# Routing the last attention batch in two halves, and ending three stages without a semaphore clear and a GpSimd drain

## The chip, the cores and the metric

The kernel is one program on one core of one Trainium2 chip. The core has TensorE (PE, with its weight loads as PEld), VectorE (DVE), ScalarE (ACT), GpSimd (POOL) and SyncE (SP), which run their own instruction streams and meet only at semaphores, and 16 DMA engines. The metric is the device time of one execution in microseconds (us), as the median of several executions; lower is better.

## The reference

Four batches (B = 4) of 1024 tokens with 256 features go through two layers. In each layer a mixer and a mixture of experts are added to the residual stream, with adaptive layer norms before them. The stages that matter here are the attention of the second layer and the routing of its experts:

```python
h = _layernorm(x) * (1 + ca) + sa
x = x + ga * _L1_attn_ref(h, Wqkv, Wo)          # 8 heads of 128, causal
h = _layernorm(x) * (1 + cb) + sb
x = x + gb * _L1_ffn_ref(h, gate_w, w1, w2)     # 16 experts, top 2, capacity 640 rows

# _L1_ffn_ref, in flat token order over all batches:
probs = jax.nn.sigmoid(xf @ gate_w.T)
top_vals, sel = jax.lax.top_k(probs, 2)
weights = top_vals / (top_vals.sum(-1, keepdims=True) + 1e-06)
ranks = (running count of each expert's tokens, in token order) - 1
valid = ranks < capacity                         # later ones are dropped
slot = jnp.where(valid, sel * capacity + ranks, sentinel)
padded = zeros.at[slot].set(x_rep)               # a row of x for each of its 2 experts
out = (gathered expert outputs * weights).sum(axis=1)
```

A token's slot depends on how many earlier tokens chose the same expert, so the tiles of 128 tokens are ranked in order.

## The kernel before

The program is five stages, each a block of its own in which every engine has its stream: the first layer's mixer (`phase_mamba`), its routing (`phase_route`), its experts (`phase_experts0`), the second layer's attention (`phase_attention`) and its experts (`phase_experts1`). A block ends with a barrier of all engines. In the built program each engine drains before the barrier, POOL among them. The semaphores of a stage are taken through the class `Semaphores`, whose exit (lines 75 and 76) has POOL drain and clear their range, and then has all engines meet at another barrier. Four single semaphores that outlive a stage (`xo_`, `rm_`, `aw_`, `ew_`) have such an object each. At the end of `phase_experts0` two ranges are cleared one after the other, at the end of `phase_attention` one, and at the program's end four.

Attention takes the batches one by one. Tokens lie in tiles of 128 on the partitions, so a batch has TPB = 8 tiles, and CT = 4 of them are half a batch. A batch's 8 heads of 8 tiles are 64 steps, in whose loop the other work has fixed places: the next batch's norms, and the routing of the previous batch (constants `R_NORM`, `R_PAIR`, `PICK`, `RANK`, `SLOTS`). After the steps come the eight output tiles (`output(t)` on PE, line 1879), which DVE scales, adds to x and takes statistics of (lines 2232 to 2236).

The last batch has no successor to hide its routing under. What follows its output tiles is, in this order:

- DVE: `variance` over 8 tiles (lines 2039 to 2045), ACT's square root (1945), `invert`, and two instructions for each of 8 rows tiles (`route_row`, lines 2059 and 2062).
- PE and ACT in turn, for each of four pairs of tiles: `turn_pair` (1797) transposes into the one bank `qk_ps`, ACT copies (1949), `logits` (1805) go into the same bank, ACT takes exp (1954). The next pair waits for that.
- DVE: `pick` twice (2082 to 2093), which gives two experts a token; PE: `count_before` (1812, 1813); DVE: `weights`, `take_ranks`, `slots` (2102 to 2121).
- POOL: 16 indirect DMAs, two for each tile, which scatter the rows into `slots1` (1757), then a wait until they have landed.

Only then does the block end and `phase_experts1` begin: SP loads the gates and the rows of expert 0 (1461, 1467), PE transposes them (1506) and works through 16 experts (1517, 1528), and POOL adds each tile of results to `out` by an indirect DMA (1494).

## Time and profile before

| | us |
|---|---|
| median of 3 timed runs | 2989.36 (2987.97 to 2989.59) |
| the profiled execution's own time | 2964.37 |
| span of its trace, first to last instruction | 2962.6 |
| last batch's output tiles end on PE | 2573.2 |
| first scatter issue of the last batch | 2607.16 |
| first instruction of the last stage | 2635.17 |
| mean granted TensorE clock over the span | 0.922 |

All rows in this text are from the one profiled execution, in us from the start of its span. The names before an instruction's operands are tiles (`at_` is attention's, `e_` the experts'), `<-` stands between what is written and what is read, and a bracket at a row's end is the time that the engine sat idle before it and what ended that. The letter q behind an engine's name stands for its instruction queue: a `DRAIN` there waits for what its engine has under way, a `COMPARE_BRANCH` or `UNCONDITIONAL_BRANCH` is the way out of a block, and it starts when the wait before it is met. The clock column PEclk gives 1.00 for 2.4 GHz and 0.50 for 1.2 GHz.

### The profile page before, as it was taken

The page shows a single profiled execution, that of the slowest core. Times are in us where ns is not written, and L with a number is a line of the kernel's source. Part 1 is how long each engine was busy: PE and PEld are TensorE (multiplying, and loading weights), DVE is VectorE, ACT ScalarE, POOL GpSimd, SP SyncE. Part 2 cuts the span into 40 slices and gives each one's busy share as a digit, 9 for nine tenths or more (in the row PEclk, how much of TensorE's full clock was granted, in tenths as well). Part 3 has the DMA queues.
Part 4 walks back from the last instruction along what each step waited for, and adds up shares of the span by engine and source line. Part 5 has one row for each costly group of instructions (what it writes and reads, how often), then busy time and mean ns, then how long its engine had stood idle before and what let it go on. Part 6 is the DMA issues. An engine that isn't in the chain of part 4 may idle for free. (4 is left out here: it accounts for less than half of the span.)

```text
span 2962.6 us, 39492 instructions
## 1 busy us (share of the span) xinstructions
PE 2504.5 (85%) x12433; PEld 1817.4 (61%) x12434; DVE 2100.9 (71%) x4243; ACT 1286.0 (43%) x2525; POOL 1241.6 (42%) x531
## 2 busy tenths in 40 slices
PE   6677877877856859998799999999999999839998
PEld 4355555555545859997466665666566666627776
DVE  4999999999998456665666567757675677435554
ACT  4667777777754215554243323323332343201111
POOL 2799999999997036665000000020002001123434
PEclk8889989988977579999799999999999999869999
DMA  4645654654654434343300010001001000035554
GB/s 145 203 152 173 198 169 168 192 175 161 200 179 149 139 112 63 63 63 53 118 1 1 1 47 1 1 30 33 1 1 47 1 1 13 32 95 127 126 128 73
DMA packets 151034, 269.21 MB, mean 91 GB/s; under 512 B 18348, under 2 KB 107484, under 8 KB 150364
## 3 DMA queue, kind: packets, MB, share of 16 engines
q1 hardware_dynamic: 121916, 227.12, 24.1%
q0 software_dynamic: 28416, 38.05, 7.8%
q10 hardware_dynamic: 544, 2.10, 0.2%
q8 instruction: 80, 1.31, 0.2%
q14 instruction: 78, 0.64, 0.1%
HBM read 209.65 MB, written 57.56 MB: 90 GB/s over the span
## 5 line engine op out<-in xcount | busy, mean ns | idle before, releaser
L765 POOL TENSOR_TENSOR dbx<-u,b_all 128x2048 f32<-128x2048 f32 x128 | 578.4, 4532 | 71.2 <-DVE u L844 34.2
L1757 POOL DMA_INDIRECT slots<-at_r_rows,slot_of x64 | 63.6, 994 | 1154.5 <-DVE slot_of L2121 1136.2
L649 ACT ACTIVATE da_ps<-delta,a_neg 128x512 f32<-128x512 f32 x512 | 347.9, 689 | 134.8 <-DVE hc L917 126.7
L1986 ACT COPY at_pt<-at_pt_ps 128x512 f32<-128x512 f32 (+3 forms) x384 | 171.8, 484 | 498.3 <-PE at_pt_ps L1858 498.1
L469 PE MATMUL y_ps<-ident,hc 128*128 128x128 f32 x1536 | 241.7, 301 | 90.8 <-DVE hc L917 90.3
L1847 PE MATMUL at_s_ps<-at_qk 128*128 128x512 f32 (+3 forms) x768 | 291.3, 489 | 3.1 <-DVE at_v L2170 3.1
L1871 PE MATMUL at_o_ps<-at_pt,at_v 128*128 128x512 f32 (+3 forms) x768 | 288.4, 487 | 0.0
L469 PEld LDWEIGHTS y_ps<-ident,hc 128*128 128x128 f32 x1536 | 196.0, 155 | 145.0 <-DVE hc L917 117.6
L1975 ACT ACTIVATE at_probs<-at_s_ps,at_small 128x128 f32<-128x128 f32 (+7 forms) x256 | 192.3, 751 | 206.2 <-DVE at_small L2181 205.8
L917 DVE TENSOR_TENSOR hc<-da_ps,c_all 128x512 f32<-128x512 f32 x384 | 257.5, 672 | 0.0
L907 DVE TENSOR_TENSOR_SCAN da_ps<-da_ps,state,dbx 128x512 f32<-128x512 f32 x192 | 243.1, 1276 | 6.1 <-ACT da_ps L649 4.3
L907 DVE TENSOR_TENSOR_SCAN da_ps<-da_ps,dbx 128x512 f32<-128x512 f32 x192 | 232.0, 1218 | 11.4 <-ACT da_ps L649 7.8
L1847 PEld LDWEIGHTS at_s_ps<-at_qk 128*128 128x128 f32 x768 | 136.9, 190 | 126.9 <-issue 94.9
L1831 PE MATMUL at_qk_ps<-at_h_b,w_qkv 128*128 128x512 f32 x448 | 211.9, 595 | 1.5 <-DVE at_rank L2107 0.9
L2177 DVE TENSOR_TENSOR at_s_ps<-at_s_ps,at_later 128x128 f32<-128x128 f32 x256 | 75.9, 296 | 186.5 <-PE at_s_ps L1847 185.5
L1494 POOL DMA_INDIRECT out<-e_ys,e_row_i x80 | 125.3, 1566 | 193.4 <-DVE e_ys L1603 164.5
L2179 DVE TENSOR_REDUCE at_small<-at_s_ps 128x1 f32<-128x128 f32 (+7 forms) x256 | 194.0, 758 | 8.8
L1858 PEld LDWEIGHTS at_pt_ps<-ident,at_probs 128*128 128x128 f32 x1152 | 136.2, 141 | 74.5 <-issue 49.6
L1858 PE MATMUL at_pt_ps<-ident,at_probs 128*128 128x128 f32 x1152 | 168.7, 273 | 11.4 <-DVE at_probs L2189 11.1
L1551 ACT ACTIVATE e_hid<-e_h_ps 128x320 f32<-128x320 f32 x128 | 56.0, 437 | 249.2 <-PE e_h_ps L1517 249.2
L1871 PEld LDWEIGHTS at_o_ps<-at_pt,at_v 128*128 128x128 f32 x768 | 127.2, 191 | 60.1 <-issue 56.6
L1528 PE MATMUL e_y_ps<-e_w,e_hid 128*128 128x256 f32 x640 | 152.3, 382 | 5.6 <-ACT e_hid L1551 5.6
(325 smaller groups left out, 5064.7 us busy)
## 6 DMA issues: line engine op xcount, KB each, us to landing
b_all<-bc_rows SPq DMA_DIRECT2D x128, 512.0 KB, 4.6
c_all<-bc_rows SPq DMA_DIRECT2D x128, 512.0 KB, 5.1
e_w<-L_ffn_w SPq DMA_DIRECT2D x32, 512.0 KB, 5.4
slots<-zeros SPq DMA_DIRECT2D x40, 260.0 KB, 6.3
e_xs<-slots SPq DMA_DIRECT2D x16, 650.0 KB, 7.1
w<-L_ffn_W SPq DMA_DIRECT2D x24, 384.0 KB, 8.6
more<-zeros SPq DMA_DIRECT2D x16, 256.0 KB, 5.2
sums<-x SPq DMA_DIRECT2D x8, 512.0 KB, 7.1
```

What stands on the lines that cost most here:

```text
L469: mm = nc.tensor.matmul(y_ps[par][:, at], source[:, at], sh.ident[:], start=False, stop=(last and j == CT - 1), is_transpose=True)
L649: nc.scalar.activation(da_ps[s % RING_DA][:], delta[:, c % 2, m, :], ACT.Exp, scale=sh.a_neg[:, m, n:n + 1]).then_inc(S["da_ready"], 1)
L765: nc.gpsimd.tensor_tensor(dbx[:, at % RING_DBX], pair, rows, ALU.mult).then_inc(S["dbx_ready"], 1)
L907: nc.vector.tensor_tensor_scan(out, h, dbx[:, at % RING_DBX, i // 2, par, :], 0.0 if c % CPB == 0 else state[:, s:s + 1], ALU.mult, ALU.ad ...
L917: nc.vector.tensor_tensor(hc[:, v % RING_H, :], da_ps[s % RING_DA][:], c_all[:, at % RING_C, s % GS // 2, :], ALU.mult).then_inc(S["hc_rea ...
L1831: last = nc.tensor.matmul(out, w_qkv[:, k, h, i // 2, :], h_b[:, i % 2, k, :], start=(k == 0), stop=(k == KE - 1))
L1847: last = nc.tensor.matmul(s_ps[n % 2][:, part * CH:end], qk[:, h % 2, 0, i * P:(i + 1) * P], qk[:, h % 2, 1, part * CH:end], start=True, s ...
L1858: last = nc.tensor.transpose(pt_ps[half][:, j % CT, :], probs[:, n % 3, j * P:(j + 1) * P], sh.ident[:])
L1871: last = nc.tensor.matmul(o_ps[:, first:], v[:, h % 2, j, :], pt[half][:, j, first:], start=(j == 0), stop=(j == (half + 1) * CT - 1))
L1975: nc.scalar.activation(probs[:, n % 3, 0:(i + 1) * P], s_ps[n % 2][:, 0:(i + 1) * P], ACT.Exp, bias=small[:, n % 4, 1:2], scale=SCALE, acc ...
L1986: nc.scalar.copy(pt[i // CT][:, half * CT:half * CT + m, at], pt_ps[half][:, 0:m, :]).then_inc(S[f"copied{half}"], 1)
L2179: nc.vector.reduce_max(small[:, n % 4, 0:1], s_ps[n % 2][:, 0:(i + 1) * P], AX_X).then_inc(S["max_taken"], 1)
```

## The change

It has two parts. The first is in `phase_attention`: `variance`, `invert`, `route_row`, `pick`, `weights`, `take_ranks` and `slots` of the last batch are replaced by functions that handle half a batch (four tiles), called `tail_*`. The first half's normalised rows, transposes and logits stand between the last output tiles; the second half follows them. Transposes go into the two banks `pt_ps`, in turn, the copies into `rows`, the logits of two pairs side by side into `qk_ps`, and the counts into `o_ps`. POOL's scatter waits for each half by itself. Three small POOL instructions prepare a constant `run_on4`. The first three batches are handled as before.

The second part: the semaphores of the last three stages and the four single ones are all taken from one object made in `program`, which clears them at the end of the program, and the blocks of these three stages are made with `no_gpsimd_drain=True`.

```diff
 program():
+        kept = ctx.enter_context(Semaphores(nc, ""))
+        sh.kept = lambda prefix: lambda name: kept(prefix + name)
-            sh.x_stored = ctx.enter_context(Semaphores(nc, "xo_"))("stored")
+            sh.x_stored = sh.kept("xo_")("stored")
...
-            sh.e0_w_in = second_block.enter_context(Semaphores(nc, "ew_"))("loaded")
+            sh.e0_w_in = sh.kept("ew_")("loaded")
 phase_experts0(), phase_experts1(), phase_attention():
-        sem = ctx.enter_context(Semaphores(nc, "at_"))
+        sem = sh.kept("at_")
-        block = ctx.enter_context(nc.Block())
+        block = ctx.enter_context(nc.Block(no_gpsimd_drain=True))
 phase_attention(), gpsimd:
-            def scatter(rb):
-                pool.wait_ge(S["slots_ready"], rb + 1)
-                for j in range(TPB):
+            def scatter(rb, tiles=range(TPB), count=None):
+                pool.wait_ge(S["slots_ready"], count or rb + 1)
+                for j in tiles:
...
-            scatter(B - 1)
+            for half in range(2):
+                scatter(B - 1, range(half * CT, (half + 1) * CT), B + half)
 tensor:
+            def tail_turn(pair):
+                pe.wait_ge(S["tail_row"], 4 * pair + 4)
+                if pair >= 2:
+                    pe.wait_ge(S["tail_copied"], pair - 1)
+                for j in range(2):
+                    for k in range(KE):
+                        last = nc.tensor.transpose(pt_ps[pair % 2][:, j * KE + k, :], r_rows[:, 2 * pair + j, k * P:(k + 1) * P], sh.ident[:])
+                last.then_inc(S["tail_turned"], 1)
+
+            def tail_logits(half):
+                if half:
+                    pe.wait_ge(S["tail_chance"], 1)
+                for pair in (2 * half, 2 * half + 1):
+                    pe.wait_ge(S["tail_copied"], pair + 1)
...
+            def tail_count(half):
+                pe.wait_ge(S["tail_masks"], half + 1)
+                if half:
+                    pe.wait_ge(S["tail_ranks"], 1)
+                pairs = both[:, half * CT:(half + 1) * CT, :]
+                nc.tensor.matmul(o_ps[:, 0:CT * NE], tri[:], pairs, start=True, stop=True)
+                nc.tensor.matmul(o_ps[:, CT * NE:2 * CT * NE], ones[:], pairs, start=True, stop=True).then_inc(S["tail_ranked"], 1)
...
                     output(t)
+                    if last_batch and t == TPB - 3:
+                        tail_turn(0)
+                    if last_batch and t == TPB - 2:
+                        tail_turn(1)
+                        tail_logits(0)
+                if last_batch:
+                    tail_count(0)
+                    tail_turn(2)
+                    tail_turn(3)
+                    tail_logits(1)
+                    tail_count(1)
 scalar:
+            for half in range(2):
+                nc.scalar.preload_act_table_set("sqrt_and_others")
+                tail_root(half)
+                nc.scalar.preload_act_table_set("exp_and_others")
+                for pair in (2 * half, 2 * half + 1):
+                    tail_copy(pair)
+                tail_chance(half)
 vector:
+                def tail_slots(half):
...
+                    tail_link(v.tensor_tensor(c, r, offs[:].rearrange("p (o e) -> p o e", o=1).broadcast_to([P, CT, NE]), ALU.add))
+                    tail_link(v.tensor_scalar(valid4, r, float(CAP1), None, ALU.is_lt))
+                    tail_link(v.scalar_tensor_tensor(out=c, in0=c, scalar=spare[:, 0:1], in1=valid4, op0=ALU.subtract, op1=ALU.mult))
+                    for k in range(2):
+                        tail_link(v.tensor_tensor(scores[:, at], mask[:, k, at], c, ALU.mult))
+                        tail_link(v.tensor_reduce(slot[:, k, at], scores[:, at], AX_X, ALU.add))
+                    tail_link(v.tensor_scalar(slot[:, :, at], slot[:, :, at], spare[:, 0:1], None, ALU.add))
+                    v.tensor_copy(sh.slot_of[:, :, b * TPB + half * CT:b * TPB + (half + 1) * CT], slot[:, :, at]).then_inc(S["slots_ready"], 1)
...
                     nc.vector.bn_stats(sh.stats[:, tile, :], sh.x[:, tile, :]).then_inc(S["stats2_in"], 1)
+                    if last_batch:
+                        if t == CT - 1:
+                            tail_variance(0)
+                        if t in (CT, CT + 1):
+                            tail_row(2 * (t - CT))
+                            tail_row(2 * (t - CT) + 1)
+                        if t == TPB - 2:
+                            tail_pick(0)
+                if last_batch:
+                    tail_variance(1)
+                    for j in range(CT, TPB):
+                        tail_row(j)
+                    tail_weights(0)
+                    tail_slots(0)
+                    tail_pick(1)
+                    tail_weights(1)
+                    tail_slots(1)
-            variance(B - 1, "2")
-            invert(B - 1, "2")
-            for j in range(TPB):
-                route_row(B - 1, j)
-            pick(B - 1, 0)
-            pick(B - 1, 1)
-            weights(B - 1)
-            take_ranks(B - 1)
-            slots(B - 1)
```

How the instructions stand now, first on TensorE from output tile 2 of the last batch to the end of the stage. `at_s_ps<-at_w_o,at_attn` is an output tile (8 matmuls), `at_r_rows` a transposed row tile, `at_gate_w` the logits, `at_tri` and `at_ones` the counts. Before:

```order
L1879 MATMUL at_s_ps<-at_w_o,at_attn 128x256 x48
L1797 MATMUL at_qk_ps<-ident,at_r_rows 128x128 x4
L1805 MATMUL at_qk_ps<-at_gate_w,at_gated 128x16 x4
L1797 MATMUL at_qk_ps<-ident,at_r_rows 128x128 x4
L1805 MATMUL at_qk_ps<-at_gate_w,at_gated 128x16 x4
L1797 MATMUL at_qk_ps<-ident,at_r_rows 128x128 x4
L1805 MATMUL at_qk_ps<-at_gate_w,at_gated 128x16 x4
L1797 MATMUL at_qk_ps<-ident,at_r_rows 128x128 x4
L1805 MATMUL at_qk_ps<-at_gate_w,at_gated 128x16 x4
L1812 MATMUL at_qk_ps<-at_both,at_tri 128x128
L1813 MATMUL at_qk_ps<-at_both,at_ones 128x128
L1632 UNCONDITIONAL_BRANCH
```

And now:

```order
L1914 MATMUL at_s_ps<-at_w_o,at_attn 128x256 x32
L1828 MATMUL at_pt_ps<-ident,at_r_rows 128x128 x4
L1914 MATMUL at_s_ps<-at_w_o,at_attn 128x256 x8
L1828 MATMUL at_pt_ps<-ident,at_r_rows 128x128 x4
L1839 MATMUL at_qk_ps<-at_gate_w,at_rows 128x16 x8
L1914 MATMUL at_s_ps<-at_w_o,at_attn 128x256 x8
L1847 MATMUL at_o_ps<-at_both,at_tri 128x64
L1848 MATMUL at_o_ps<-at_both,at_ones 128x64
L1828 MATMUL at_pt_ps<-ident,at_r_rows 128x128 x8
L1839 MATMUL at_qk_ps<-at_gate_w,at_rows 128x16 x8
L1847 MATMUL at_o_ps<-at_both,at_tri 128x64
L1848 MATMUL at_o_ps<-at_both,at_ones 128x64
```

The transposes of the first pair stand ahead of output tile 6, those of the second pair and the logits of both ahead of output tile 7, and each half has its counts.

Second, DVE around the last output tile (`at_gated<-at_s_ps,mods` takes it, `BN_STATS` ends it). Before:

```order
L2232 TENSOR_TENSOR at_gated<-at_s_ps,mods 128x256
L2234 TENSOR_TENSOR x<-x,at_gated 128x256
L2236 BN_STATS stats<-x 128x6
L2232 TENSOR_TENSOR at_gated<-at_s_ps,mods 128x256
L2234 TENSOR_TENSOR x<-x,at_gated 128x256
L2236 BN_STATS stats<-x 128x6
L2039 TENSOR_TENSOR mean<-stats 128x8
L2040 TENSOR_SCALAR mean<-mean 128x8
```

And now, from the fourth row before it:

```order
L2325 SCALAR_TENSOR_TENSOR at_cand<-at_cand,at_iota_e 128x64
L2326 TENSOR_REDUCE at_idx<-at_cand 128x4
L2327 TENSOR_TENSOR at_mask<-at_iota_e,at_idx 128x64
L2331 TENSOR_TENSOR at_both<-at_mask 128x64
L2376 TENSOR_TENSOR at_gated<-at_s_ps,mods 128x256
L2378 TENSOR_TENSOR x<-x,at_gated 128x256
L2380 BN_STATS stats<-x 128x6
L2293 TENSOR_TENSOR mean<-stats 128x4
L2294 TENSOR_SCALAR mean<-mean 128x4
```

The first half's 14 instructions of `pick` (the last four are shown) stand between output tiles 6 and 7, and the statistics are those of four tiles.

Third, POOL from the last batch's scatter to the end of the program's stages. `L75 ISA` is the clear of a range of semaphores, a branch the end or the start of a block. Before, from the end of attention:

```order
L1632 UNCONDITIONAL_BRANCH [waits ss_own_kept]
L75 ISA [waits barrier_Pool_Activation_PE_DVE_SP_gather]
L1482 UNCONDITIONAL_BRANCH [waits barrier_Pool_Activation_PE_DVE_SP_gather]
L1484 IOTA e_expert 128x16
L1486 IOTA e_spare 128x5
```

And now, from the first half's last seven scatters (the semaphore's number has another first owner, whose name is shown):

```order
L1763 DMA slots<-at_r_rows,slot_of 10368x260 x7
L1763 DMA slots<-at_r_rows,slot_of 10368x260 [waits ss_zeros_set]
L1763 DMA slots<-at_r_rows,slot_of 10368x260 x7
L1632 UNCONDITIONAL_BRANCH [waits ss_ident_set]
L1482 UNCONDITIONAL_BRANCH [waits barrier_Pool_Activation_PE_DVE_SP_gather]
L1484 IOTA e_expert 128x16
L1486 IOTA e_spare 128x5
```

The clear between the two branches has gone, as have the two at the end of `phase_experts0`; at the program's end one `L75 ISA` stands where there were four. That clear keeps the drain of POOL that comes with it (line 75).

## Rows read from the trace of the kernel before

**Rows 1.** Windows: us, busy time (instructions) by engine, clock, DMA share, GB/s.
```profile
2540.00:2573.00 33.00, 33.00 (x144) 26.82 (x142) 9.63 (x22) 0.60 (x1) 0.00 (x0) 1.00 0.00 0
...
2601.00:2642.00 41.00, 0.01 (x1) 0.01 (x1) 6.32 (x23) 1.28 (x1) 15.59 (x18) 0.50 0.27 94
2642.00:2657.00 15.00, 14.23 (x44) 9.31 (x44) 8.70 (x28) 3.12 (x8) 0.00 (x0) 0.72 0.59 196
```

**Rows 2.** Timeline, end of attention: start, us, engine, line, instruction, idle before it.
```profile
2573.22 0.42 DVE L2232 TENSOR_TENSOR at_gated<-at_s_ps,mods 128x256 f32<-128x256 f32 x1 [2.11 <-PE at_s_ps L1879]
...
2574.60 0.17 DVE L2039 TENSOR_TENSOR mean<-stats 128x8 f32<-128x8 f32 x1
...
2576.57 0.48 DVE L2059 SCALAR_TENSOR_TENSOR at_r_rows<-x,mean,mods 128x256 f32<-128x256 f32 x1
...
2583.51 0.48 DVE L2062 SCALAR_TENSOR_TENSOR at_r_rows<-at_r_rows,rstd,mods 128x256 f32<-128x256 f32 x1
...
2594.40 0.23 DVE L2082 TENSOR_SCALAR at_chances<-at_chances 128x128 f32<-128x128 f32 x1 [10.40 <-ACT at_chances L1954]
2594.66 0.95 DVE L2083 RECIPROCAL at_chances<-at_chances 128x128 f32<-128x128 f32 x1
...
2599.21 0.29 DVE L2093 TENSOR_TENSOR at_both<-at_mask 128x128 f32<-128x128 f32 x1
...
2601.10 0.29 DVE L2102 COPY at_plus<-at_qk_ps 128x128 f32<-128x128 f32 x1
...
2606.71 0.17 DVE L2121 CAST slot_of<-at_slot 128x16 uint32<-128x16 f32 x1
2607.16 0.96 POOL L1757 DMA_INDIRECT slots<-at_r_rows,slot_of  x1 [78.34 <-DVE slot_of L2121]
...
2626.12 0.96 POOL L1757 DMA_INDIRECT slots<-at_r_rows,slot_of  x1 [0.30 <-issue]
```

**Rows 3.** Line 1632, attention's block end: queue records, ns min/median/max, start.
```profile
L1632 POOLq COMPARE_BRANCH  x1: 43/43/43, 2628.7 to 2628.7; - x1
L1632 POOLq DRAIN  x1: 5279/5279/5279, 2628.8 to 2628.8; - x1
...
L1632 SPq EVENT_SEMAPHORE  x1: 17/17/17, 2634.3 to 2634.3; - x1
```

**Rows 4.** Line 1224, the block end of `phase_experts0`.
```profile
L1224 POOLq COMPARE_BRANCH  x1: 44/44/44, 1400.8 to 1400.8; - x1
L1224 POOLq DRAIN  x1: 4464/4464/4464, 1400.9 to 1400.9; - x1
```

**Rows 5.** Line 1421, the block end of `phase_experts1`.
```profile
L1421 POOLq COMPARE_BRANCH  x1: 41/41/41, 2956.3 to 2956.3; - x1
L1421 POOLq DRAIN  x1: 4137/4137/4137, 2956.5 to 2956.5; - x1
```

**Rows 6.** Timeline, starts of the last two stages.
```profile
1406.93 0.37 SPq L1697 DMA_DIRECT2D x<-sums  x1
...
2635.17 0.34 SPq L1461 DMA_DIRECT2D mods<-mod_rows  x1
...
2639.43 1.10 DVE L1610 TENSOR_TENSOR mods<-mods 128x256 f32<-128x256 f32 x3 [32.55 <-DMA mods<-mod_rows]
```

**Rows 7.** Line 75, the nine semaphore clears, each with its drain.
```profile
L75 POOLq DRAIN  x9: 41/89/174, 973.3 to 2962.2; - x9
L75 POOLq EVENT_SEMAPHORE_RANGE_CLEAR  x9: 44/131/461, 973.5 to 2962.2; - x9
```

**Rows 8.** Timeline, TensorE routing a pair inside the last batch, at clock 1.00.
```profile
2465.00 0.60 PE L1797 MATMUL at_qk_ps<-ident,at_r_rows 128*128 128x128 f32 x4
2466.94 0.96 PE L1805 MATMUL at_qk_ps<-at_gate_w,at_gated 128*128 128x16 f32 x8
```

**Rows 9.** Timeline, first and last of 16 scatter issues while DVE is busy.
```profile
2508.51 0.96 POOL L1757 DMA_INDIRECT slots<-at_r_rows,slot_of  x1 [266.28 <-DVE slot_of L2121]
...
2527.86 0.96 POOL L1757 DMA_INDIRECT slots<-at_r_rows,slot_of  x1 [0.30 <-issue]
```

More of the change, by code:

```diff
@@ L1651, in phase_attention @@
         r_turned = gated[:].rearrange("p j (k t) -> p j k t", k=KE)
+        tail_rows = rows[:].rearrange("p (h j) (k t) -> p h j k t", h=2, k=KE)
         s_ps = [ps(f"s_ps{i}", [P, T]) for i in range(2)]
@@ L1928, in batch @@
                     output(t)
-            batches(pe, batch)
-            for pair in range(PAIRS):
-                if pair:
-                    pe.wait_ge(S["chances_ready"], (B - 1) * PAIRS + pair)
-                turn_pair(B - 1, pair)
-                logits(B - 1, pair)
-            pe.wait_ge(S["chances_ready"], B * PAIRS)
-            count_before(B - 1)
+                    if last_batch and t == TPB - 3:
[9 more added lines that the diff above has]
+                    tail_count(1)
+            batches(pe, batch)
         @block.scalar
@@ L2005, in _, with tail_root, tail_copy, tail_chance @@
             batches(act, batch)
-            root(B - 1, "2")
-            for pair in range(PAIRS):
-                copy_pair(B - 1, pair)
-                chance(B - 1, pair)
+            def tail_root(half):
+                act.wait_ge(S["tail_var"], half + 1)
+                at = slice((B - 1) * TPB + half * CT, (B - 1) * TPB + (half + 1) * CT)
+                nc.scalar.activation(sh.var[:, at], sh.var[:, at], ACT.Sqrt).then_inc(S["tail_std"], 1)
+            def tail_copy(pair):
+                act.wait_ge(S["tail_turned"], pair + 1)
+                if pair >= 2:
+                    act.wait_ge(S["tail_logits"], 1)
+                nc.scalar.copy(tail_rows[:, pair % 2], pt_ps[pair % 2][:].rearrange("p (j k) t -> p j k t", j=2)).then_inc(S["tail_copied"], 1)
+            def tail_chance(half):
+                act.wait_ge(S["tail_logits"], half + 1)
+                at = slice(half * CT, (half + 1) * CT)
+                nc.scalar.activation(chances[:, at, :], qk_ps[:, 0:CT * NE].rearrange("p (j e) -> p j e", j=CT), ACT.Exp, scale=-1.0).then_inc(S["tail_chance"], 1)
+            for half in range(2):
[5 more added lines that the diff above has]
+                tail_chance(half)
         @block.vector
```

98 lines of the change are left out of this document (90 added, 8 removed).

## The prediction

> **What bounds the kernel now.** The span is a chain of five stages, so I read first, by windows, what each engine does around the last stage change. Up to 2573 TensorE is busy for all of 33.00 us at a granted clock of 1.00 (2.4 GHz). From 2601 to 2642 it does nothing for 41 us, while POOL is busy for 15.59 us [rows 1]. So the attention stage is bound by TensorE until its last output tile, and from there to the first matmul of the last stage time goes by a chain of small steps. The timeline shows it in order. DVE takes the last output tile at 2573.22, begins `variance` at 2574.60, writes rows from 2576.57 to 2583.99, then sits idle for 10.40 us until the fourth pair's logits are there, picks experts from 2594.40 to 2599.50, takes ranks and slots from 2601.10 to 2606.88, and POOL scatters from 2607.16 to 2627.08, 16 issues at a spacing of (2626.12 - 2607.16) / 15 = 1.264 us [rows 2]. The queue records tell what comes next: POOL's wait for the landing is met at 2628.7, its drain takes 5.279 us, the others pass the barrier at 2634.3 [rows 3], and SP starts the last stage at 2635.17 [rows 6]. POOL's drain has nothing of the kernel left to wait for, since the landing is behind it. The two other stage ends have the same form, with drains of 4.464 and 4.137 us after 1400.8 and 2956.3 [rows 4, 5].
>
> **Part one, the routing.** I go along the new order with the old durations.
>
> TensorE. DVE spends 1.34 us on an output tile and then waits 2.11 for the next [rows 2], so they come every 3.45 us, the last at 2573.2 and tile 5 at 2566.3. The transposes of pair 0 wait for rows 0 and 1. DVE has finished tile 4 by 2564.2; inverting and two rows at (2583.99 - 2576.57) / 8 = 0.93 us each end at 2566.4 [rows 2], just after tile 5. A pair's transposes and logits take 0.60 and 0.96 us at clock 1.00 [rows 8], about 0.44 and 0.88 of which hold the engine up when more stands behind. So tile 6 runs from 2566.9 to 2570.4, pair 1 is turned by 2571.0, both pairs' logits are done at 2572.8, tile 7 at 2576.3, 3.1 us later than now. Nobody but DVE waits for tile 7.
>
> DVE. Exp of the first half is there at 2573.1. `pick` is now 14 instructions in 5.10 us, 13 of them 0.29 us long (0.325 apart) and a reciprocal of 0.95 [rows 2]. A row of 8 elements takes 0.17, one of 128 takes 0.29, so by the line between them one of 64 takes about 0.22 (0.255 apart), and the reciprocal 0.55: half a `pick` is 3.9 us, and ends at 2577.0. Then tile 7 (1.4 us) to 2578.4, variance 1.45 and root and inversion 0.55 to 2580.4, four rows 3.7 to 2584.1, `weights` 1.7 (as now, small instructions do not shrink) to 2585.8, `tail_slots`, 15 instructions, 3.8 to 2589.6. POOL starts 0.3 later, at 2589.9, against 2607.16: **17.3 us earlier**.
>
> Second half. It must not come later than POOL's ninth issue, at 2589.9 + 8 x 1.264 = 2600.0. TensorE has had little to do since 2576.3 and its clock is at 0.50 by then, as it is now from 2601 [rows 1]. At that level a pair's logits take about twice 0.88; turned after row 7 (2584.1), both pairs' exp is there at 2589.0, before DVE is free at 2589.6. Then pick 3.9, weights 1.7, slots 3.8: 2599.0, 1.0 us in time. Issues run without a gap and the last ends at 2609.9.
>
> DVE now works beside the first 8 issues. Where that is so today, 16 issues go from 2508.51 to 2528.82, 20.31 us [rows 9], against 19.92 in the quiet tail [rows 2]. So I charge 0.3 us. By the Trainium skill (SBUF — State Buffer, "A bandwidth-pool intuition that's wrong") a GpSimd DMA of some 620 ns takes some 3100 when a DVE copy holds the shared port; the trace does not agree for these instructions, all but one of the issues there being 0.96 us long or near it. **The routing saves 17.0 us.**
>
> Bounds: if instructions on 64 elements cost as much as on 128, picks are 5.1 and slots 5.6; POOL starts at 2592.9, the second half is ready at 2605.0 instead of 2603.0 and the end is 12 us earlier than now. If they cost as little as those on 8 (0.2 apart), POOL starts 1.8 us earlier yet: 18.8. I take 17.0, by the line between the rows.
>
> What else moves: SP's store of x waits for tile 7 and is issued at 2578 instead of 2574; it is waited for only at the block's end, over 30 us later. ACT has two table loads more (1 before `root`, 1 before the copies of each half), each while it waits for DVE's rows. POOL's three new instructions are at the stage's start, ahead of the first batch's norms.
>
> **Part two, the stage ends.** What remains between POOL's met wait and the next stage is the way to the barrier and through it; in rows 3 the others pass 0.2 us after the drain's end (2634.1). I count 0.3 in all.
>
> - `phase_experts0` to attention: now 1400.8 to 1406.93 is 6.1 us [rows 4, 6], of it 4.5 drain and 1.6 two clears and three barriers. Left 0.3 to 0.6, **5.7 saved** (5.5 to 5.8).
> - Attention to the last stage: 2628.7 to 2635.17 is 6.4 [rows 3, 6], left 0.3, **6.1 saved**.
> - Program end: 2956.3 to the span's end at 2962.6 is 6.3. Here the barrier is followed at once by the one clear that is kept, and that clear brings its own drain of POOL. The nine drains at clears take 41 to 174 ns now, because each has a full drain ahead [rows 7]; without it I expect this one to take the 4.0 us that are left of the 4.1. The clears take 44 ns (one semaphore) to 461 (78) [rows 7], 5.4 ns for each; 109 take 0.63. With barriers 0.6: 0.3 + 4.0 + 0.63 + 0.3 = 5.2, so **1.1 saved**. Bounds: 0.5, and 5.2 if the drain is short after all.
>
> Does a drain left out come back as a slower POOL in the next stage? No row shows it. Its cover is there: in the last stage POOL makes two constants that DVE wants once its gates are in, 4.3 us after the start [rows 6], and with 5.3 us of hidden drain they would be 1 us late. In attention POOL's constants are wanted only after the first rows are loaded and normalised. So nothing to 1 us; I take nothing.
>
> **The sum.** 17.0 + 5.7 + 6.1 + 1.1 = 29.9 us. The profiled execution took 2964.37 (a span of 2962.6 and 1.8 around it), so it would take 2934.5. The timed runs' median is 25.0 higher, 2989.36, for reasons that the trace does not show; I take the difference over as it is: **2959.5 us**, 1.0% faster.
>
> **The rivals.**
>
> 1. *The last drain goes too.* As above but the drain at the clear is short. For it: at clears it always was. Against it: all nine had another just ahead. 4.1 less: 2955.4.
> 2. *The second half is the bound.* Narrow instructions don't get cheaper, and POOL waits between the halves for `slots_ready`. For it: below 128 elements a fixed part dominates (0.17 at 8, 0.29 at 128 [rows 2]); the margin is only 1.0 us. 5 us less of the gain: 2964.5.
> 3. *The drains' time comes back at the barrier.* POOL's queue can't pass the barrier's semaphore until what the drain waits for is over. The two stage ends give back 4.5 and 5.3: 2969.3. For it: 5.3 us after the landing POOL still had something to finish. Against: nothing else waits for it.
> 4. *DVE locks POOL out.* The first 8 issues get no turn while `pick`, `weights` and `slots` of the second half run (9.4 us), so scattering starts in effect at 2599.0: 9.1 later, 2968.6. Rows 9 speak against it; the page on SBUF named above for it.
> 5. *Slower: TensorE stays at 1.2 GHz into the last stage.* That stage is bound by TensorE, 14.23 us busy of its first 15, at a mean clock of 0.72 [rows 1]; it starts at 0.50 after the idle stretch and rises within this window. If, with that stretch cut from 41 to some 24 us, the rise came much later, every us of matmuls at half clock costs 1 more. It turns the sign once 29.9 us of matmul work more than now run at 0.50; with 40 us the time is 2959.5 + 40 = 2999.5. Against it: the clock rose within 10 us of steady work here, and a shorter idle stretch before it gives no reason for a later rise.
> 6. *It doesn't do what it says*, for a wait of the new code ends late and the first half's scatter starts no earlier than the second's would: only part two is left, 2976.
>
> **Chances.** Forecast 0.70 (its own range 2956.5 to 2963.5), rival 1 0.10, rival 2 0.08, rival 3 0.05, rival 4 0.02, rival 5 0.02, rival 6 0.02, no change in sum for any other reason 0.01. The range goes from 2953, a little below rival 1, to 2969, which takes in rivals 2 and 4 and most of 3. A measurement of this kernel can tell a difference of about 0.2%, 6 us. All but rival 5 and the rest are beyond it: faster 0.95, within 0.02, slower 0.03.
>
> **What would show it.** In the new trace, where everything behind the first stage end stands 5.7 us earlier: the first scatter issue of the last batch at about 2584.2, and none later than 2603; no gap over 0.5 us between the eighth issue and the ninth; no POOL drain at lines 1224, 1632 and 1421, and at line 75 one of about 4 us behind the last barrier; the next stage's first DMA within 0.5 us of POOL's met wait, twice. A gap before the ninth issue makes rival 2 right, a barrier 4 us after the met wait rival 3, issues of 3 us rival 4. If the sum of these holds and the timed median is more than 6 us off 2959.5, then what stands between profiled and timed runs has changed, and the step that took it over is wrong.

## The result, and the profile after

| | before | after | difference |
|---|---|---|---|
| median of 7 timed runs each, us | 2988.76 | 2952.82 | -35.9 |
| profiled execution, its own time | 2964.37 | 2951.45 | -12.9 |

The ratio of the timed runs is 0.9901 (95% interval 0.9882 to 0.9920): faster by 0.8 to 1.2%. The forecast was 2959.5 us, 29.9 less than before, in a range of 2953 to 2969; the median lies just outside its lower end. Five of the seven runs after took 2951.5 to 2953.1, two 2972.7 and 2973.1. The ratio lies nearer to one than that of the medians (0.9880) because these two weigh in it: the averages, 2988.0 and 2958.2, are 29.8 apart. So this comparison alone gives 30 to 36 us; the repeats below give 32 to 36. The two traces differ by far less than the medians, and most of that gap is not the change's: the experiments were needed to part the two.

**The end of attention.** In the trace of after the last batch's first output tile starts at 2555.15, where before it started at 2539.72, so I compare distances from there. The timeline of after (start, us, engine, line, instruction, idle before it), answering to [rows 2]:

```profile
2588.05 0.22 ACT L2058 ACTIVATE at_chances<-at_qk_ps 128x64 f32<-128x64 f32 x1 [1.16 <-PE at_qk_ps L1839]
...
2591.95 0.22 DVE L2331 TENSOR_TENSOR at_both<-at_mask 128x64 f32<-128x64 f32 x1
2592.09 0.42 DVE L2376 TENSOR_TENSOR at_gated<-at_s_ps,mods 128x256 f32<-128x256 f32 x1
...
2595.32 0.48 DVE L2310 SCALAR_TENSOR_TENSOR at_r_rows<-x,mean,mods 128x256 f32<-128x256 f32 x1
...
2603.50 0.22 ACT L2058 ACTIVATE at_chances<-at_qk_ps 128x64 f32<-128x64 f32 x1 [2.64 <-PE at_qk_ps L1839]
...
2604.75 0.17 DVE L2369 CAST slot_of<-at_slot 128x8 uint32<-128x8 f32 x1
...
2605.19 0.96 POOL L1763 DMA_INDIRECT slots<-at_r_rows,slot_of  x1 [77.24 <-DVE slot_of L2369]
...
2614.04 0.96 POOL L1763 DMA_INDIRECT slots<-at_r_rows,slot_of  x1 [0.30 <-issue]
2614.12 0.17 DVE L2369 CAST slot_of<-at_slot 128x8 uint32<-128x8 f32 x1
2615.31 0.96 POOL L1763 DMA_INDIRECT slots<-at_r_rows,slot_of  x1 [0.30 <-issue]
...
2624.16 0.96 POOL L1763 DMA_INDIRECT slots<-at_r_rows,slot_of  x1 [0.30 <-issue]
```

POOL starts 2605.19 - 2555.15 = 50.0 us after the first output tile; in [rows 2] it was 2607.16 - 2539.72 = 67.4. The eighth issue is followed by the ninth without a gap, and the second half's slots were there at 2614.3, 1.0 us ahead of the ninth issue at 2615.31. The last issue starts 69.0 us after the first output tile, before it was 86.4: 17.4 less.

**The ends of the stages.** The queue records of attention's end and of the program's end (ns min/median/max, start), answering to [rows 3, 5, 7]:

```profile
L1632 POOLq COMPARE_BRANCH  x1: 37/37/37, 2626.7 to 2626.7; - x1
L1632 SPq EVENT_SEMAPHORE  x2: 17/17/17, 2597.7 to 2627.0; - x2
...
L1421 POOLq COMPARE_BRANCH  x1: 41/41/41, 2948.2 to 2948.2; - x1
...
L75 POOLq DRAIN  x3: 106/174/209, 975.6 to 2948.6; - x3
L75 POOLq EVENT_SEMAPHORE_RANGE_CLEAR  x3: 177/461/629, 975.8 to 2948.8; - x3
```

There is no POOL drain any more at lines 1224, 1632 and 1421. From POOL's met wait to the barrier it is 0.3 us. The last clear takes 0.63 us, as worked out, but its drain takes at most 0.21, not 4.0. From the start of the next stages (answering to [rows 6]):

```profile
1379.77 0.37 SPq L1700 DMA_DIRECT2D x<-sums  x1
...
2627.03 0.34 SPq L1461 DMA_DIRECT2D mods<-mod_rows  x1
...
2631.20 1.09 DVE L1610 TENSOR_TENSOR mods<-mods 128x256 f32<-128x256 f32 x3 [16.91 <-DMA mods<-mod_rows]
```

SP's first DMAs come 0.37 us (POOL's wait was met at 1379.4) and 0.33 us after the met waits. The last stage starts as before with TensorE at the lower clock, and the clock rises within the same window as in [rows 1] (0.72 there). Windows of after (us, busy time by engine in the order PE, PEld, DVE, ACT, POOL, clock, DMA share, GB/s):

```profile
2555.00:2588.00 33.00, 32.83 (x153) 26.86 (x154) 14.47 (x38) 3.69 (x5) 0.00 (x0) 1.00 0.00 0
2588.00:2626.70 38.70, 10.79 (x49) 9.19 (x48) 22.35 (x93) 4.39 (x7) 15.35 (x16) 0.59 0.24 82
2626.70:2633.30 6.60, 0.00 (x0) 0.00 (x0) 1.09 (x3) 1.28 (x1) 0.24 (x2) 0.50 0.72 234
2633.30:2648.30 15.00, 14.19 (x42) 9.29 (x43) 8.70 (x28) 3.06 (x7) 0.00 (x0) 0.69 0.61 206
```

**What else differs between the two traces.** By stage, from one block's barrier to the next (us):

| | mixer | routing 1 | experts 1 | attention | experts 2 |
|---|---|---|---|---|---|
| before | 973.2 | 106.4 | 326.3 | 1228.4 | 326.5 |
| after | 975.5 | 83.1 | 321.1 | 1247.3 | 321.5 |

The first routing stage is untouched and yet 23.3 us shorter; attention has lost over 20 us at its ends and yet is 18.9 longer. The first is TensorE's clock. The same 56 us of that stage, before and after:

```profile
976.00:1032.00 56.00, 53.41 (x251) 53.41 (x251) 27.20 (x66) 12.80 (x36) 0.59 (x5) 0.50 0.43 143
```

```profile
979.00:1035.00 56.00, 33.95 (x260) 32.97 (x260) 45.10 (x112) 14.27 (x38) 3.52 (x1) 0.74 0.75 244
```

In before's profiled execution the clock stayed at 0.50 (1.2 GHz) through 53 us of busy TensorE; after's rose to 1.00 (2.4 GHz) within 10 us of the stage's start. The second lies within batches: output tiles follow at 289.6, 289.8 and 283.2 us before, at 302.4, 303.7 and 299.1 after, in code that was not changed. The extra 42.6 us sit in the three stretches where POOL scatters a batch's rows beside the next batch's steps. The waits of after from 2200 to 2235 (us in total, times, longest):

```profile
ACT at_pt L2024 <- remote: 11.7, 3, 8.1
...
DVE at_rows L2200 <- remote: 4.2, 1, 4.2
...
DVE at_attn L2250 <- remote: 3.8, 1, 3.8
```

The word `remote` marks waits whose end no record explains. The trace of before has none of them. I call these stretches the stops.

### The profile page after: what moved, and what is told of

The parts are those of the page before. It is cut to its first block, busy times and chain, and to the rows that moved or that the text cites. A ratio compares the mean times of both kernels' runs of the same rounds, so it can differ in the third digit from the quotient of the medians.

```text
span 2949.8 us, 39479 instructions
## 1 busy us (share of the span) xinstructions
PE 2499.3 (85%) x12437; PEld 1806.4 (61%) x12438; DVE 2106.9 (71%) x4284; ACT 1287.8 (44%) x2526; POOL 1241.5 (42%) x533
## 4 chain that ended last, share of the span: by engine, by line
PE 44%; DVE 3%; issue 2%; ACT 1%; another core or an unknown queue 1%; DMA 1%; POOL 0%; SPq 0%; DVEq 0%; ACTq 0%; POOLq 0%
PE at_o_ps L1906 8%; PE at_s_ps L1882 8%; PE at_qk_ps L1866 6%; PE e_h_ps L1517 5%; PE e_y_ps L1528 5%; PE at_s_ps L1914 4%; PE at_pt_ps L1893 4%; PE at_qk_ps L1871 3%; PE at_s_ps L1866 1%; DVE at_small L2236 1%; PE e_x_ps L1506 0%; PE at_s_ps L1871 0%; DMA at_w_o<-woT 0%; PE at_qk_ps L1812 0%
## 5 line engine op out<-in xcount | busy, mean ns | idle before, releaser
L1906 PE MATMUL at_o_ps<-at_pt,at_v 128*128 128x512 f32 (+3 forms) x768 | 294.3, 495 | 0.0
L1893 PE MATMUL at_pt_ps<-ident,at_probs 128*128 128x128 f32 x1152 | 171.5, 276 | 33.7 <-ACT at_pt L2024 14.2
L774 POOL TENSOR_TENSOR own_h<-own_h,c_all 128x2048 f32<-128x2048 f32 x32 | 144.7, 4523 | 31.2 <-DVE own_h L907 31.2
```

The source lines that it names most:

```text
L1893: last = nc.tensor.transpose(pt_ps[half][:, j % CT, :], probs[:, n % 3, j * P:(j + 1) * P], sh.ident[:])
L1906: last = nc.tensor.matmul(o_ps[:, first:], v[:, h % 2, j, :], pt[half][:, j, first:], start=(j == 0), stop=(j == (half + 1) * CT - 1))
```

## The experiments

Twelve runs in four series. A series is a set of kernels that took turns on one chip within some minutes, with runs of before among them. Medians in us; `e4`, `e8`, `e11` are the changed kernel again, `e3` is before again.

| series | before | kernels |
|---|---|---|
| 1 | 2943.72 | e1 2927.39, e2 2926.34, e3 2944.31, e4 2909.80 |
| 2 | 2983.63 | e5 2968.59, e7 2958.00, e8 2951.69, e6 2988.73 (one run) |
| 3 | 2984.16 | e9 2909.38, e10 2951.72, e11 2947.95 |
| 4 | 2944.39 | e12 2943.34 |

**The whole change, and before, once more.** No edit.

> The kernel before once more, for its trace and the clock and span of its timed runs. Its first trace is 25 us shorter than its timed median. Theory A: TensorE's clock and some waits differ between executions; this trace will show a time between 2983 and 2990 us, and at least one of two things: the first routing stage at full clock (83 us and not 106), or waits of PE, ACT and DVE for one another of some 14 us during each batch's scatter inside attention, as in the trace of after, with batches 302 us apart and not 290. Rival B: the timed runs are longer outside the span (before its first or behind its last instruction): the span of the timed runs stays at 2963.

> The changed kernel once more. Its timed runs fell into two groups, five at 2951.5 to 2953.1 and two at 2972.7 and 2973.1. Theory A: the groups differ by the first routing stage's clock, worth 23 us in the two traces so far; the first group comes again in most runs, and batches stand 302 us apart in its trace. Rival B: the groups differ by the waits during the scatters (14 us each): then a trace of the faster group has batches 290 us apart in at least one place.

> The changed kernel beside the three others on the same chip. By the runs so far the difference to before is 34 to 36 us on either chip, whichever level before stands at (2944 or 2988 us). If before stands near 2988 here, the trace shows the waits of ACT, DVE and PE during the three scatters inside attention, with batches 299 to 304 us apart; if near 2944, none, and batches 283 to 290 us apart.

> The changed kernel beside these two. Before at 2944 or at 2984 to 2989 tells which of the two levels this chip has; the changed kernel is 34 to 36 us under it on either, and its trace has the waits in the scatters only on the slower one.

Before stands at one of two levels 40 us apart, 2944 or 2984 (2988.76 in the first comparison), and keeps it for a whole series. The changed kernel is 33.9, 31.9 and 36.2 us under it (ratios 0.9879, 0.9886, 0.9883). All seven traces taken at the upper level without the edit of e9 have the stops (after, e5 to e8, e10, e11), with batches 296 to 304 us apart; the four of series 1 have none (e4: 289.9, 290.3, 283.2), and before's first trace is of that kind. I wrote of "one chip" and "the other" in some expectations: the chip numbers of the series don't bear this out, each of the two numbers was there once with either level. What sets the level is open.

For e3 both of my readings were wrong as written. Its timed runs took 2942.4 to 2945.4, but its profiled execution took 2968.05, for it had the slow first routing stage (106.3 us, clock 0.50) that few timed runs have (among the 23 of before in this series one, 2964.15). For e4, no run of the longer group came again (2908.9 to 2912.9), and its trace has the first routing stage at the normal clock; batches 302 apart, the other half of theory A, did not come, since this series had no stops. That a slow first routing stage makes an execution some 23 us longer is shown by the traces of e3 (2968.05 against 2944.31) and e5 (2991.82 against 2968.59); the two long runs of after have no trace.

So before's profiled execution had run at the lower level with a slow routing stage, and its timed runs at the upper level with a normal one: 2964.37 - 23.3 + 42.6 = 2983.7, and 5 us to the median of 2988.76 remain unexplained. They are in the spread of the upper level (2983.6, 2984.2, 2988.8).

**Part one alone** (e1): the changed kernel with this undone.

```diff
-        kept = ctx.enter_context(Semaphores(nc, ""))
-        sh.kept = lambda prefix: lambda name: kept(prefix + name)
-        sem = sh.kept("at_")
-        block = ctx.enter_context(nc.Block(no_gpsimd_drain=True))
+        sem = ctx.enter_context(Semaphores(nc, "at_"))
+        block = ctx.enter_context(nc.Block())
... (the same for the other semaphores and blocks)
```

> The first part of the change alone: the last batch is routed in two halves, while all semaphore clears and POOL's drains stand as before. Theory A (the two parts add up, and nothing else has moved): from the last batch's first output tile to the last scatter issue 69.1 us instead of 86.4, so 17.3 less; the stage ends keep their drains of 4 to 5 us; the timed median is 17 us under before's. Rival B (most of the 35.9 us between the medians comes from other places, such as TensorE's clock in the first routing stage, 23.2 us less in the trace of after, and the two parts are worth less): 5 to 10 us. Rival C (the parts depend on each other, the drain behind the scatter grows when routing is earlier): attention's drain is 7 us or more in place of 5.3, and 15 us or less are gained.

Measured: 16.3 us under before by the medians (ratio 0.9947, 0.9929 to 0.9964). From the first output tile to the last issue it is 2587.11 - 2518.44 = 68.7 us, before 86.4, and to the barrier 76.9, before 94.6: 17.7 less in both. POOL's drain is 5279 ns, as in [rows 3]. Theory A holds, rivals B and C are out.

**Part two alone** (e2): before with the edit of e1 turned round.

> The second part of the change alone: semaphores kept to the end and no drain of POOL at three block ends, while the last batch is routed as before. Theory A (the parts add up, by the trace of after): first experts to the first transposes of attention 4.9 less, attention to the first transposes of the last stage 6.6 less of which 6.1 stay, program end 4.7 less; 15.7 in all. The prediction had 12.9 for this, with a drain of 4.0 us kept at the last clear. Rival B (drains come back in the next stage): 5 us or less. The drain at the last clear is 0.1 to 0.3 us long in the trace by theory A, 4 us by the prediction.

Measured: 17.4 us under before (ratio 0.9930, 0.9907 to 0.9952), so by the medians the parts add up: 16.3 + 17.4 = 33.7 against 33.9 for both (each ratio is known to some 5 to 7 us). The last drain is 0.19 us or less here too, where the routing is before's. This is more than the 15.7 I gave theory A, because I had put the start of attention down with 4.9 (its first transposes come 23.0 and 18.2 us after the met wait). The 0.9 lost there is made up: from SP's first DMA to the first output tile it is 270.2 us before and 270.1 after.

**The drains without the kept semaphores** (e5): before, and only this in three places.

```diff
-        block = ctx.enter_context(nc.Block())
+        block = ctx.enter_context(nc.Block(no_gpsimd_drain=True))
```

> Before with POOL's block-end drain left out of the last three blocks and nothing else: each stage's semaphores are still cleared at its end (two ranges, one, and four), every clear with its own small drain of POOL just ahead of it. It tells what the drains are worth and what the clears are. Theory A (the drain in a clear is short by nature, 0.05 to 0.3 us, as it was at the program's end of the changed kernel): the stage ends lose 4.46, 5.28 and 4.14 us, 13.9 in all, less 0.8 given back at attention's start: 13 us under before. Rival B (the prediction's step: a drain in a clear has to do the full drain's work where none stands ahead): the drain of the first clear of each stage end becomes 4 to 5 us long and the time stays within 3 us of before.

Measured: 15.0 us less (ratio 0.9947, 0.9934 to 0.9961). Nine clears stand as before, seven of them now without a full drain ahead:

```profile
L75 POOLq DRAIN  x9: 41/77/229, 973.7 to 2989.7; - x9
L75 POOLq EVENT_SEMAPHORE_RANGE_CLEAR  x9: 44/131/461, 973.9 to 2989.7; - x9
```

The longest drain in a clear takes 0.23 us. Rival B, which was the prediction's step, is out at all three places. The drains carry most of part two. The clears that are no longer made, with their barriers, are worth about 2 us by the medians (17.4 - 15.0, in different series), and 2.7 by the traces: from POOL's met wait to SP's first DMA of the next stage, or to the end of the span, it is 1.7, 1.2 and 2.1 us in e5, and 0.4, 0.4 and 1.5 in e2.

**What the drain is** (e6): before, with POOL kept busy between landing and block end.

```diff
             pool.wait_ge(S["scattered"], 2 * TILES * 16)
+            for h in range(HEADS):
+                nc.gpsimd.memset(attn[:, h, :], 0.0).then_inc(consts, 1)
```

> Before with eight POOL memsets of 128x1024 added between the landing of attention's last scatter and the block's end; they overwrite a tile that nobody reads any more. It tells what attention's drain of 5.28 us is. Theory A (it is a fixed piece of work, since 5.279 us came out to the ns in four traces): it stays at 5.28 us, and the stage end is longer by the memsets' whole time. Rival B (it waits for something that goes on behind the landing): it is shorter by the memsets' time, and the stage end grows by that time less 5.28 at most.

The timeline has the memsets, the queue records the drain:

```profile
2646.48 7.20 POOL L1768 MEMSET at_attn<- 128x1024 f32 x8 [1.53 <-DMA slots<-at_r_rows,slot_of]
```

```profile
L1632 POOLq DRAIN  x1: 12520/12520/12520, 2646.5 to 2646.5; - x1
```

The drain is taken up at once, waits out the memsets (7.20) and then takes another 12.52 - 7.20 = 5.32 us, against 5.28 without them. The barrier stands 2659.2 - 2646.48 = 12.7 us behind the start of the memsets, in before 5.5 behind the start of the drain: the stage end is longer by the memsets' whole time. The record of the drain is not 5.28 us long, as theory A said, for it counts the memsets in. So 7.2 us of other work hid none of it: rival B is out. The drain is not a wait for what the landing left behind but a piece of its own behind POOL's last instruction here. That its length is the same to 4 ns in all traces that have it (4464, 5279, 4133 or 4137 at the three places) fits. What it does is open.

**What the split of the scatter is worth** (e7): the changed kernel, with one wait later.

```diff
-                scatter(B - 1, range(half * CT, (half + 1) * CT), B + half)
+                scatter(B - 1, range(half * CT, (half + 1) * CT), B + 1)
```

> The changed kernel, but POOL starts the last batch's scatter only once the slots of both halves are ready; nothing else is changed. It parts the 17.3 us of the routing into what comes from scattering beside the second half and what comes from routing earlier. Theory A: slots of the second half are ready 9.1 us after those of the first; the first issue comes at that point, the last issue starts 9.1 us later than in the changed kernel, and the time is 9.1 us more than the changed kernel's, by trace and by median. Rival B (POOL's 8 issues in between hold DVE and PE up, so without them the second half is ready earlier): less than 8 us more.

Measured by trace: first issue 2610.25 - 2551.05 = 59.2 us after the first output tile, 9.2 later than in after, and the last issue as much later, so theory A holds by the trace. By medians it is 6.3 more than e8 in the same series, which would be rival B's less than 8; against before the ratios are 0.9913 and 0.9886, 2.7 thousandths or 8.1 us apart. The stops of this series blur the medians (batches 295.9 to 302.2 apart in e7, 299.3 to 303.5 in e8). By the traces about half of the routing's 17.4 us comes from scattering beside the second half, and the rest from the new order of the routing itself (the first half between the output tiles, two pairs' transposes and logits without a wait between pairs), which no run parts further.

**TensorE kept warm over the stage end** (e10).

```diff
+                    for i in range(WARM_END):      # 80, behind tail_count(1)
+                        nc.tensor.transpose(pt_ps[i % 2][:, i // 2 % CT, :], sh.ident[:], sh.ident[:])
...
+            for i in range(WARM_START):            # 36, ahead of turn_x(0, ...)
+                nc.tensor.transpose(y_ps[i % 2][:, 0:P], sh.ident[:], sh.ident[:])
... (in phase_route)
-        sem = ctx.enter_context(Semaphores(nc, "rt_"))
+        sem = sh.kept("rt_")
-        block = ctx.enter_context(nc.Block())
+        block = ctx.enter_context(nc.Block(no_gpsimd_drain=True))
```

> The changed kernel with 80 transposes of the identity, which nobody reads, on TensorE behind the last counts of attention and 36 more at the last stage's start ahead of its wait for rows, and with the first routing stage's semaphores kept and its end without POOL's drain too. Theory A (the last stage starts at 1.2 GHz only because TensorE did nothing for 23 us before it): its first transposes and first 32 matmuls run at 2.4 GHz, 10.5 us of hidden layer become 8.8 and 3.0 of transposes 1.9, 2.8 us less; the kept semaphores give 1.0 more; 3.8 us under the changed kernel. Rival B (the transposes end too late and hold the barrier or the first rows up): PE passes the barrier after POOL, and the time is as before or longer.

Measured: 2951.72, 3.8 us above e11 rather than below it (the four runs of e10 spread over 7 us). TensorE reached the barrier 5 us after POOL (2631.0 against 2626.0), as rival B has it, and the clock fell all the same: it was 1.00 at 2636 to 2638, TensorE was busy for 2.6 us of the 5.6 between its last added transpose and the hidden layer, and the clock was 0.50 again from 2641 to 2645, where the hidden layer's first 32 matmuls took 10.95 us (11.51 in e11) and not 8.8. But the run shows something else. These 80 transposes wait for no semaphore, and POOL scatters from 2604.6 to 2624.9. The timeline of TensorE:

```profile
2609.13 6.28 PE L1981 MATMUL at_pt_ps<-ident 128*128 128x128 f32 x46
2615.84 0.38 PE L1981 MATMUL at_pt_ps<-ident 128*128 128x128 f32 x2 [0.42 <-issue]
2617.26 0.27 PE L1981 MATMUL at_pt_ps<-ident 128*128 128x128 f32 x1 [1.04 <-issue]
...
2622.89 0.80 PE L1981 MATMUL at_pt_ps<-ident 128*128 128x128 f32 x3 [1.62 <-issue]
2625.01 0.37 PE L1981 MATMUL at_pt_ps<-ident 128*128 128x128 f32 x1 [1.33 <-issue]
...
2627.14 3.78 PE L1981 MATMUL at_pt_ps<-ident 128*128 128x128 f32 x17 [0.52 <-issue]
```

46 transposes run without a gap in 6.28 us. From 11 us after the scatter's first issue until its landing they come by ones and twos, with up to 1.6 us between them and nothing to wait for. So a stop is not, or not only, a signal that comes late: TensorE itself does not get on. One thing that it could lack, though it waits for no semaphore, is its instructions: the profile has two DMA queues for them, q8 and q14. No experiment took this up. The one block of 16 KB that q8 moved in this stop took 1.21 us, and such blocks take 0.88 to 1.45 in the attention of e4, which has no stops, so the move itself is not slower; what goes before it isn't recorded.

**The stops themselves** (e9): the changed kernel, POOL letting each DMA land.

```diff
                                                      in_=r_rows[:, j, :], in_offset=None).then_inc(S["scattered"], 16)
+                        if rb < B - 1:
+                            pool.wait_ge(S["scattered"], (2 * i + k + 1) * 16)
```

> The changed kernel, but the scatters of the first three attention batches (those beside the next batch's steps) go one at a time: POOL waits for each of the 16 DMAs to land before it issues the next. On one chip ACT, DVE and PE lose some 14 us to one another in each of these three scatters, from about 8 us after its first issue until its last write has landed at 22; on the other chip they lose nothing. Theory A (signals between engines come late because scatter DMAs follow each other without a pause): on the chip with the waits batches stand 290 us apart in place of 302 and the time falls by 30 to 42 us against the changed kernel; on the other chip it stays within 2 us. Rival B (what counts is the whole time in which a scatter is under way): it gets longer, from 20 to some 60 us, and so do the waits: 20 us or more slower on the chip with the waits.

Measured, in a series at the upper level: 2909.38 us (2907.70 to 2911.01), 38.6 under e11 and 74.8 under before (ratio 0.9751, 0.9737 to 0.9764). Batches stand 289.9, 290.2 and 283.2 us apart, and no wait ends on `remote`. POOL in the second batch's scatter:

```profile
1906.59 1.04 POOL L1763 DMA_INDIRECT slots<-at_r_rows,slot_of  x1 [522.50 <-DVE slot_of L2180]
1909.36 1.09 POOL L1763 DMA_INDIRECT slots<-at_r_rows,slot_of  x1 [1.73 <-DMA slots<-at_r_rows,slot_of]
1912.22 0.96 POOL L1763 DMA_INDIRECT slots<-at_r_rows,slot_of  x1 [1.77 <-DMA slots<-at_r_rows,slot_of]
```

An issue every 2.9 us in place of 1.27 makes the scatter last 45 us instead of 21, and nobody waits for it. Theory A's numbers hold for a series in this state, and rival B is out: it is not the time under way. Whether it is the rate or the number of DMAs under way at once is not shown, since the wait changes both.

**The same on before** (e12), same edit.

> Before, with the first three attention batches' scatters paced as in e9 (POOL waits for each DMA to land before the next) and nothing else. Theory A (the stops in the scatters are a matter of their own, on one chip only): on the chip with the stops, 38 to 42 us under before, batches 283 to 290 us apart in the trace; on the other chip, where before takes 2944 us, within 3 us of before. Rival B (the pacing costs something that the chip with the stops hides): on the chip without them it is 3 us or more slower than before.

This series was at the lower level: 2943.34 against 2944.39 (ratio 1.0003, 0.9979 to 1.0027), so where there is nothing to win the pacing costs nothing that this comparison can tell (0.2%, some 6 us), and rival B has nothing for it. Before with pacing at the upper level was not run.

## Why the prediction was right, and where it was not

The direction and the mechanism were right, except for the last drain; the size was 6.0 us too small by the medians. Its terms, each against the traces:

| term | predicted | measured |
|---|---|---|
| routing | 17.0 | 17.4 |
| first experts to attention | 5.7 | 5.8 |
| attention to the last stage | 6.1 | 6.1 |
| program end | 1.1 | 4.7 |
| sum | 29.9 | 34.0 |

- **Routing, the chain.** Set against the first output tile (15.4 us later than in the trace of before), every step was met within 0.7 us: exp of the first half done 2588.3 (predicted 2573.1 + 15.4 = 2588.5), `pick` 2592.2 (2592.4), rows 2599.1 (2599.5), slots 2604.9 (2605.0), second exp 2603.7 (2604.4), second slots 2614.3 (2614.4). TensorE's output tiles end 3.0 us later, predicted 3.1. The durations on 64 elements, taken from the line between 8 and 128, came out as 0.22 and the reciprocal as 0.55, as estimated. Two small misreadings did not matter: 12 instructions of `pick` take 0.29 us in the old trace, not 13 (the first takes 0.23), and POOL's new constant takes two instructions, not three.
- **Beside DVE.** The 0.3 us charged for DVE beside POOL's first issues was not needed: the spacing is (2624.16 - 2605.19) / 15 = 1.265 us, in [rows 2] 1.264. That disposes of rival 4. What I did not see is that its mechanism is there on a small scale. Of the 64 issues in the trace of before five take 1.21 to 1.34 us, the others 0.96 to 1.09, and each of the five starts while DVE's `TENSOR_SCALAR` of line 2189 runs on 768 to 1024 elements, as the long one behind [rows 9]:

```profile
2515.85 0.75 DVE L2189 TENSOR_SCALAR at_probs<-at_probs,at_small 128x1024 f32<-128x1024 f32 x1
2516.10 1.34 POOL L1757 DMA_INDIRECT slots<-at_r_rows,slot_of  x1 [0.30 <-issue]
```

  Not every issue that starts in one is long (one at 2513.57 takes 0.96). By the Trainium skill (SBUF — State Buffer, "A bandwidth-pool intuition that's wrong") a GpSimd DMA beside a DVE copy waits until DVE releases the shared port. These five go that way, by at most 0.4 us; whether line 2189 holds that port is not recorded, and no issue here is five times as long, as the DMA on that page is.
- **Rival 2** did not happen: no gap before the ninth issue, with the margin of 1.0 us that was worked out.
- **Stage ends.** No drain comes back, neither at the barrier (rival 3: it stands 0.3 us behind the met wait) nor in the next stage (POOL's constants were there 4 us before DVE wanted them). e6 fits this: the drain there was not waiting for work still under way.
- **The step that failed** is the program end: "that clear brings its own drain of POOL ... without it I expect this one to take the 4.0 us". It takes 0.21. I had the right rows [rows 7] and read against them, since all nine had a full drain ahead; e5 shows that it made no difference. This is rival 1, given 0.10, with 4.1 us; the term is mis-sized by 3.6, and with it the forecast would have been 2955.9. The sign named in advance for it, a drain of about 4 us at line 75, is not there.
- **The 25.0 us taken over** between the profiled execution and the timed runs. As numbers for after's own trace it gave 2934.5 us and a first scatter issue at 2584.2; they are 2951.45 and 2605.19, and trace and median are 1.4 us apart, not 25.0. The prediction had also said that a median more than 6 us off 2959.5, with its sum met, makes this step wrong. The median is 6.7 off, but the sum was not met: 4.1 of the 6.7 are in its terms and 0.6 in before's own median (2989.36 then, 2988.76 now). So as a step of the sum it held to 2 us, because what makes it up, stops in three scatters less a slow routing stage, is in neither part of the change, and both kernels were timed at the same level. It was a step without a reason, and it is luck of the comparison rather than insight that it did no harm: against the 2909.80 of series 1 the same forecast is 49.7 us off, though the difference to before is the same 33.9.
- **Rival 5** (TensorE's clock stays low in the last stage) did not happen: clock 0.69 in its first 15 us against 0.72, and the stage from SP's first DMA to POOL's last met wait takes 2948.2 - 2627.0 = 321.2 us, before 2956.3 - 2635.2 = 321.1.

The remaining 1.9 us between 34.0 and 35.9 are less than what the series differ by (31.9 to 36.2).

The version that beats both is the changed kernel with paced scatters (e9), 2909.38 us where before takes 2984.16 and the changed kernel 2947.95. At the lower level the changed kernel takes 2909.80 without the pacing (e4), and e9 was not run there.

## What to carry to other kernels

A chain of small steps can be forecast to some tenths of a us from the rows of the old code, instruction by instruction, if the waits between engines are counted too. When a profiled execution and the timed runs are 25 us apart, lay a second trace of the same kernel beside it, stage by stage, before adding anything up: the difference can sit in code that nobody is changing, and can be worth more than the change. Scatters that are off the critical path need not go as fast as POOL can issue them; ask what they do to the engines beside them (here it paid 38.6 us in a series at the upper level, and nothing in before at the lower one).

## What the runs showed of the hardware

- POOL's block-end drain costs 4.1 to 5.3 us though all its DMAs have landed, and at attention's end 5.3 us also when 7.2 us of other work have passed (e6); the drain that comes with a semaphore clear costs 0.04 to 0.23 us, with or without a full one ahead (e5).
- Where a series stands at the upper level, 16 indirect DMAs issued every 1.27 us hold up TensorE, ScalarE and VectorE for 9 to 16 us in all, from about 8 us after the first issue (11 in e10) until the last has landed; one at a time, an issue in 2.9 us, they don't (e9). TensorE stands still even with instructions that wait for nothing (e10). POOL goes on issuing through a stop, 0.96 to 1.03 us each (after, 2215 to 2227). Neither what sets the level nor what TensorE lacks there is settled.
- In some executions (the traces of before, e3 and e5) TensorE stays at 1.2 GHz through 51 to 53 us of busy time in 56 us of the first routing stage, which then takes 106 us and not 83 (before against after).
- An indirect DMA issue of 0.96 us can take up to 1.34 when it starts beside a VectorE `TENSOR_SCALAR` on 768 to 1024 elements (before, five of 64).
